# Six waits of TensorE, each preceded by 2 to 7 matmuls of the mask with the identity

## The chip, the cores and the metric

The kernel runs on one core of one Trainium2 chip. The metric is the device time in microseconds (us) of one execution; less is better. In the profile, PE is TensorE's matmuls, PEld its weight loads, DVE is VectorE, ACT is ScalarE, POOL is GpSimd and SP is SyncE.

## The reference

The input is `x` of 16 sequences (called b below) of 256 positions and 128 channels, fp32. Four layers follow one another. Each normalises x and adds two branches to it.

```python
# layer 0
x1 = mqa(xn) + xn                      # 16 heads of 8, one shared k and v, causal softmax
y  = mamba(x1)                         # conv over 4 steps, h = dA*h + dBu, y = sum_n h*C, gate, w_out
x  = x + (y + x1) + experts0(xn)       # 32 experts, each takes its 8 best positions
# layer 1
x  = x + attention(xn) + ffn(xn)       # 16 heads of 64; silu(fp4(x)@fp4(wg)) * (fp4(x)@fp4(wu)), then fp4(.)@fp4(wd)
# layer 2
x  = x + attention(xn) + switch(xn)    # 16 heads of 8; one of 8 experts for each position, with a capacity
# layer 3
x  = x + context(ssm_scan(xn)) + moe(xn)
```

## The kernel before

**The order of the work.** For each layer a Python program writes the queue of every engine by hand. A stage is a generator that yields a slot number before each piece of work, and `merge` puts the pieces of several stages into one queue in the order of their slots. One round of this is a turn, and a turn works on several sequences at once: in layer 0, turn t holds `pe_pre0(t+2)` (normalised input, gate, q, k, v), `pe_wide0(t)` (the scores of t and the row maxima of t+1), `pe_out(t-1)` and `pe_inner(t-1)` (output projection and the first half of mamba), `pe_states(t-2)` (the scan) and `pe_results(t-3)` (mamba's output). Layer 2 has turns of `pe_pre2`, `pe_wide` and `pe_out`; layer 1 has turns of attention, `pe_ffn` and the next sequence's projections. Each engine runs its queue in order and waits on semaphores; `wait_ge` leaves out a wait that its queue has already seen.

**Scores.** `pe_quad` makes the scores of four groups of heads at once, in two slots of two PSUM banks each, from operands with 8 rows (for the maxima, L569) or 9 rows (for the exponentials, L573: the ninth row carries the negated maximum). It then adds the causal mask by multiplying it with the identity into the same bank, in bf16 (L578 for the maxima, L580 for the keys). `k.slot_read` and `pe_take` (with `k.pre_read`) hold the event after which a bank may be written again.

**The six places.** In each, TensorE waits first or also for the bank, and then for operands.

- `pe_pre0`, slot 46 (layer 0): the bank is free when DVE has read q (L967); the operand is `gv`, the gate's values. Then L270 transposes them.
- `pe_quad` with the keys, first of three (layer 2): the bank is free after `mxT` was read by ACT (L1796), the operand is the negated maximum, which a DMA carries into the ninth row of q (`negmax`). Then L573.
- `pe_max_turn` (layer 2): the operand is the last of the row maxima `mx` (DVE, L1308). Then L597 turns them.
- `pe_pv`, half 0 (layer 0): the operands are the exponentials `pt` (ACT, L1787). Then L617 multiplies them with v.
- `pe_results` (layer 0): the operand is `yT` (DVE, L1452). Then L784 multiplies it with `w_out`.
- `pe_ffn`, q = 0 (layer 1): the operand is `xqT` (ACT, L1934). Then L832 and L833 make gate and up.

Two further pieces of layer 0 matter below. `pe_sums` (L761) adds the scan's states with the identity as weights, 16 matmuls on fp32 data that the trace shows in records of 256 columns each. DVE's products (L1417) write the scan's input from what L748 spreads, into the tiles that L761 reads.

Of the kernel before, what the change touches and what calls it, by code (L numbers as in the profile page):

```python
# [236 lines left out]
    return k.bank[PRE_BANK[l]]  # L237


def pe_pre0(k, b):  # L240
    pe, w = k.pe, k.w
    xn, xnT = k.xn[b % 3], k.xnT[b % 2]
    yield 17.2
    bk = pe_take(k, 0)
    pe.wait_ge(*k.at("xn", 0, b))
    for q in range(QT):
        i = pe.e.transpose(bk[:, q * P:(q + 1) * P], xn[:, q, :], w["ident"])
    i.then_inc(*k.set("xn_turned", 0, b))
    k.pre_read = ("xnT", 0, b)
    yield 18.6  # L250
    bk = pe_take(k, 0)
    pe.e.matmul(bk[0:E0, 0:L], w["gate_w"], xnT[:, :], start=True, stop=True).then_inc(*k.set("gate", b))
    k.pre_read = ("gz", b)
    yield 24
    bk = pe_take(k, 0)
    for g in (0, 1):
        i = pe.e.matmul(bk[:, g * L:(g + 1) * L], w["wq0"][:, g, :], xnT[:, :], start=True, stop=True)
    i.then_inc(*k.set("qk", 0, b, 0))
    k.pre_read = ("qk_act", 0, b, 0)
    yield 41  # L260
    bk = pe_take(k, 0)
    for g in (2, 3):
        i = pe.e.matmul(bk[:, (g - 2) * L:(g - 1) * L], w["wq0"][:, g, :], xnT[:, :], start=True, stop=True)
    i.then_inc(*k.set("qk", 0, b, 1))
    k.pre_read = ("qk_ve", 0, b, 1)
    yield 46
    bk = pe_take(k, 0)
    pe.wait_ge(*k.at("gv", b))
    for q in range(QT):
        i = pe.e.transpose(bk[:, q * E0:(q + 1) * E0], k.PT[:, b, q * P:(q + 1) * P], w["ident"][0:E0, 0:E0])  # L270
    i.then_inc(*k.set("gv_turned", b))
    k.pre_read = ("gvT", b)
    yield 48
    bk = pe_take(k, 0)
    for q in range(QT):
        i = pe.e.matmul(bk[:, 0:E0], xn[:, q, :], k.gvT[:, q, :], start=q == 0, stop=q == QT - 1)
    i.then_inc(*k.set("merged_mm", b))
    k.pre_read = ("merged", b)
    yield 51.1
    bk = pe_take(k, 0)  # L280
    pe.e.matmul(bk[:, 0:L], w["wk0"][:, 0, :], xnT[:, :], start=True, stop=True)
    for q in range(QT):
        i = pe.e.matmul(bk[:, L + 8 * q:L + 8 * q + 8], xnT[:, q * P:(q + 1) * P], w["wv0"], start=True, stop=True)
    i.then_inc(*k.set("v_mm", 0, b, 1))
    k.pre_read = ("v", 0, b)
# [262 lines left out]
def pe_quad(k, l, kind, b, c):  # L548

    pe, w, qT, kT = k.pe, k.w, k.qT[b % 3], k.kT[b % 3]  # L550
    slots, groups = quad_slots(l, kind, b, c), quad_groups(kind, c)
    nh = len(groups)
    wid = 512 // nh
    for s in slots:
        if k.slot_read[s] is not None:
            pe.wait_ge(*k.at(*k.slot_read[s]))
    if c == 0 and kind == "max":
        pe.wait_ge(*k.at("qk_act", l, b, (len(QK[l]) - 1) // 2 * 2))
        pe.wait_ge(*k.at("qk_ve", l, b, len(QK[l]) // 2 * 2 - 1))
        pe.wait_ge(*k.at("v", l, b))  # L560
    if c == 0 and kind == "keys":
        pe.wait_ge(*k.at(f"negmax{b % 2}", l, b))
    banks = [k.bank[2 * slots[r // 2] + r % 2] for r in range(4)]
    for n, g in enumerate(groups):
        for r in range(4):
            cols, kg, row = slice(n * wid, (n + 1) * wid), g if l else 0, 32 * r
            if kind == "max":
                q0 = P if nh == 2 else 0
                pe.e.matmul(banks[r][:, cols], qT[row:row + 8, g, q0:q0 + P], kT[row:row + 8, kg, 0:wid],  # L569
                            start=n == 0, stop=True, skip_group_check=True)  # L570
            else:
                k0 = 0 if nh == 2 else P
                pe.e.matmul(banks[r][:, cols], kT[row:row + 9, kg, k0:k0 + P], qT[row:row + 9, g, k0:L],  # L573
                            start=n == 0, stop=True, skip_group_check=True)
    for r in range(4):
        v3 = banks[r].rearrange("p (n x) -> p n x", n=nh)
        if kind == "max":
            i = pe.e.matmul(v3[:, :, wid - P:wid], w["identb"], w["mask"][:, 0:nh * P], start=False, stop=True, skip_group_check=True)  # L578
        else:
            i = pe.e.matmul(v3[:, :, 0:P], w["identb"], w["maskT"][:, 0:nh * P], start=False, stop=True, skip_group_check=True)  # L580
    i.then_inc(*k.set("quad_" + kind, l, b, c))
    for h in range(2):
        k.slot_read[slots[h]] = ("mx" if kind == "max" else "exp", l, b, c, h)
# [7 lines left out]
def pe_max_turn(k, l, b):  # L591
    pe = k.pe
    s = quad_slots(l, "keys", b, 0)[0]
    pe.wait_ge(*k.at(*k.slot_read[s]))
    pe.wait_ge(*k.at("mx", l, b, 2, 1))
    for q in range(QT):
        i = pe.e.transpose(k.bank[2 * s][0:HEADS, q * P:(q + 1) * P], k.mx[b % 2][:, q, :, :].rearrange("p r g -> p (r g)"), k.w["ident"])  # L597
    i.then_inc(*k.set("mx_turned", l, b))
    k.slot_read[s] = ("mxT", l, b)


def pe_pv(k, l, b, half):

    pe, v, bk = k.pe, k.v[b % 3], k.bank[OUT_BANK[l]]
    c = 2 * half
    pe.wait_ge(*k.at("exp", l, b, c, 1))
    pe.wait_ge(*k.at("exp", l, b, 1, 1))
    if half:
        pe.wait_ge(*k.at("oU", l, b, 0))
    elif b:  # L610
        pe.wait_ge(*(k.at("x1", l, b - 1) if l else k.at("zc", b - 1, 1)))
    for kb in range(2):
        for n in range(2):
            for r in range(4):
                g, o = 2 * half + n, (r % 2) * 512
                pt = k.pt[2 * c + r // 2][:, o + n * L:o + (n + 1) * L] if kb == 0 else k.pt[2 + r // 2][:, o + g * P:o + (g + 1) * P]
                i = pe.e.matmul(bk[32 * r:32 * r + 32, n * L + kb * P:(n + 1) * L], v[:, kb, 4 * g + r if l else 0, :], pt,  # L617
                                start=kb == 0 and n == 0, stop=kb == 1, tile_position=(0, 32 * r), skip_group_check=True)
    i.then_inc(*k.set("pv", l, b, half))
# [156 lines left out]
def pe_results(k, b):  # L776

    pe, w = k.pe, k.w
    yield 13.1
    bk = pe_take(k, 0)  # L780
    pe.wait_ge(*k.at("yT", b))
    for q in range(QT):
        for c in range(CI):
            i = pe.e.matmul(bk[:, q * P:(q + 1) * P], k.yT[:, c, q * P:(q + 1) * P], w["w_out"][:, c, :], start=c == 0, stop=c == CI - 1)  # L784
    i.then_inc(*k.set("y_out", b))
    k.pre_read = ("x_mamba", b)
# [26 lines left out]
def pe_ffn(k, b):  # L813
    pe, w = k.pe, k.w
    B6, B7 = k.bank[6], k.bank[7]
    yield 12.6
    pe.wait_ge(*k.at("fp4", "x", b))
    if b:
        pe.wait_ge(*k.at("x_ffn", b - 1))
        pe.wait_ge(*k.at("hqT", b - 1, 2))  # L820
    for q in range(QT):
        i = pe.e.transpose(B7[:, q * P:(q + 1) * P], k.xq[:, q, :], w["ident"])
    i.then_inc(*k.set("xq_turned", b))
    for q in range(QT):
        yield GATE1[q]
        if q == 0:
            pe.wait_ge(*k.at("xqT", b))
            if b == 0:
                pe.wait_ge(*k.at("x_spread", 1))
        else:  # L830
            pe.wait_ge(*k.at("hh", b, q - 1))
        pe.e.matmul(B6[:, 0:I1], k.xqT[:, q * P:(q + 1) * P], k.wgT[:, :], start=True, stop=True).then_inc(*k.set("gate1", b, q))  # L832
        pe.e.matmul(B7[:, 0:I1], k.xqT[:, q * P:(q + 1) * P], k.wuT[:, :], start=True, stop=True).then_inc(*k.set("up1", b, q))  # L833
    for ch in range(3):
        yield HQ1[ch]
        rows, bk = min(P, I1 - ch * P), B6 if ch % 2 == 0 else B7
        pe.wait_ge(*k.at("fp4", "h", b))
        if ch == 0 and b + 2 < NB:
            pe.wait_ge(*k.at("x_spread", b + 2))
        if ch == 2:  # L840
            pe.wait_ge(*k.at("hqT", b, 0))
        for q in range(QT):
            i = pe.e.transpose(bk[0:rows, q * P:(q + 1) * P], k.hq[:, q, ch * P:ch * P + rows], w["ident"])
        i.then_inc(*k.set("hq_turned", b, ch))
    yield 46
    pe.wait_ge(*k.at("hqT", b, 2))
    for q in range(QT):
        for ch in range(3):
            rows = min(P, I1 - ch * P)
            i = pe.e.matmul(B7[:, q * P:(q + 1) * P], k.hqT[0:rows, ch, q * P:(q + 1) * P], k.wdT[0:rows, ch, :], start=ch == 0, stop=ch == 2)  # L850
    i.then_inc(*k.set("down1", b))
# [1787 lines left out]
```

## Time and profile before

| | before |
|---|---|
| time, median of 3 runs | 3434.24 us (3432.38 to 3438.52) |
| span of the profiled execution | 3436.0 us |
| TensorE matmul busy (PE) | 2682.7 us, 78% |
| VectorE busy (DVE) | 2233.3 us, 65% |
| ScalarE busy (ACT) | 1430.7 us, 42% |
| GpSimd busy (POOL) | 834.9 us, 24% |
| mean granted TensorE clock | 0.812 |

The profiled execution has no time of its own beside its span of 3436.0 us, which is 1.8 us above the median of the runs and within their range. Layer 0 lies between about 30 and 1150 us of the span, its experts until about 1340, layer 1 until about 2270, layer 2 until about 2870, and layer 3 ends the span. A busy share of PE says how long matmuls were in flight, not how fast they ran: the same matmul is in flight for longer when the granted clock is low. [...]

### The profile page before, as it was taken

Reading aid. Unit: us, or ns where it says so; the run is one execution under the profiler, and the core shown is the slowest. Engines: PE = TensorE matmul, PEld = TensorE weight load, DVE = VectorE, ACT = ScalarE, POOL = GpSimd, SP = SyncE. Lnnn points to the kernel's source line nnn. Section 1 sums busy time; section 2 is a strip of 40 time slices with the busy share of each in tenths; the row PEclk is TensorE's granted clock in tenths of the full one; section 3 lists DMA queues with packets and bytes.
Section 4 is the critical chain, followed back from the end, with each engine's and each line's share of the span. In section 5 each row is a group of like instructions: output and inputs, shape, how many; then the busy total and the mean of one; then the engine's idle time right before and its main releaser. Section 6 shows DMA issues by size and latency. Waiting matters only on the chain.

```text
span 3436.0 us, 46802 instructions
## 1 busy us (share of the span) xinstructions
PE 2682.7 (78%) x17705; PEld 1913.2 (56%) x17705; DVE 2233.3 (65%) x4585; ACT 1430.7 (42%) x3688; POOL 834.9 (24%) x453
## 2 busy tenths in 40 slices
PE   4788888888886876878787877758888886677776
PEld 2466666666655774555555555535565555445444
DVE  3478888887878333656666666644544533899887
ACT  1334434434444003555555555512332323444443
POOL 0033333333344200222222222210000000333332
PEclk9778778778788656899989999966777768888887
DMA  1001100110101430000000000000000002443442
GB/s 54 20 32 34 36 32 30 40 32 26 44 32 44 137 141 1 1 1 1 1 1 1 1 1 1 1 33 17 25 17 12 6 16 63 148 144 125 149 137 87
DMA packets 71345, 147.93 MB, mean 43 GB/s; under 512 B 6864, under 2 KB 37072, under 8 KB 70608
## 3 DMA queue, kind: packets, MB, share of 16 engines
q1 hardware_dynamic: 69072, 140.73, 12.5%
q0 software_dynamic: 2048, 4.20, 0.4%
q8 instruction: 141, 2.31, 0.3%
q14 instruction: 84, 0.69, 0.1%
HBM read 135.20 MB, written 9.18 MB: 42 GB/s over the span
## 4 chain that ended last, share of the span: by engine, by line
PE 32%; DVE 15%; issue 12%; ACT 8%; POOL 5%; DMA 1%; SPq 0%; DVEq 0%; POOLq 0%; ACTq 0%
POOL h L2033 4%; ACT pr L1743 3%; PE psum L569 2%; PE psum L573 2%; PE psum L497 2%; PE psum L340 2%; DVE mx L1264 2%; PE psum L761 2%; PE psum L508 2%; PE psum L463 2%; PE psum L318 2%; PE psum L809 2%; PE psum L580 2%; PE psum L799 2%; PE psum L578 1%
## 5 line engine op out<-in xcount | busy, mean ns | idle before, releaser
L1999 POOL TENSOR_TENSOR h<-h,Crep 128x1024 f32<-128x1024 f32 x128 | 383.2, 3004 | 759.5 <-DVE h L1426 759.5
L1981 POOL TENSOR_TENSOR pr<-pr,rsum 128x512 f32<-128x512 f32 x192 | 228.0, 1191 | 756.2 <-DVE rsum L1276 756.2
L1308 DVE TENSOR_REDUCE mx<-psum 128x4 f32<-128x1024 f32 (+1 forms) x192 | 229.0, 1216 | 121.5 <-PE psum L578 121.5
L761 PE MATMUL psum<-h,pack_wf 128*128 128x256 f32 x1024 | 290.8, 448 | 5.4 <-POOL h L1999 5.4
L1426 DVE TENSOR_TENSOR_SCAN h<-dA,h 128x1024 f32<-128x1024 f32 x128 | 290.8, 2286 | 2.4 <-ACT dA L1884 1.8
L761 PEld LDWEIGHTS psum<-h,pack_wf 128*128 128x128 f32 x1024 | 236.5, 236 | 54.5 <-POOL h L1999 6.4
L1787 ACT ACTIVATE pt<-psum 128x1024 f32<-128x1024 f32 x192 | 187.4, 1021 | 146.5 <-PE psum L580 142.4
L1417 DVE TENSOR_TENSOR h<-dtu,psum 128x512 f32<-128x512 f32 x256 | 164.4, 676 | 117.1 <-PE psum L748 71.0
L2033 POOL TENSOR_TENSOR h<-h,Crep 128x1024 f32<-128x1024 f32 x64 | 150.6, 2354 | 350.2 <-DVE h L1185 350.2
L1743 ACT ACTIVATE pr<-psum,nb 128x256 f32<-128x256 f32 (+1 forms) x512 | 211.9, 441 | 31.2 <-DVE nb L1268 31.2
L1884 ACT ACTIVATE dA<-delta,A 128x255 f32<-128x255 f32 x512 | 210.2, 495 | 12.1 <-DVE h L1426 10.7
L395 PE MATMUL psum<-h,pack_wf 128*128 128x256 f32 x512 | 149.9, 444 | 55.5 <-POOL h L2033 54.8
L1753 ACT ACTIVATE prT<-psum 128x512 f32<-128x512 f32 x192 | 115.0, 599 | 181.2 <-PE psum L477 180.5
L573 PE MATMUL psum<-qT,kT 9*128 9x256 f32 (+1 forms) x2048 | 150.6, 439 | 50.1 <-DMA qT<-mxT 30.3
L313 PE MATMUL psum<-xnT,pack_wf 128*128 128x256 f32 x512 | 154.8, 429 | 21.6 <-ACT qT L1646 14.9
L569 PE MATMUL psum<-kT,qT 8*128 8x128 f32 (+1 forms) x2048 | 151.1, 432 | 25.9 <-ACT pt L1787 17.3
L395 PEld LDWEIGHTS psum<-h,pack_wf 128*128 128x128 f32 x512 | 106.5, 218 | 88.7 <-POOL h L2033 73.7
L573 PEld LDWEIGHTS psum<-qT,kT 9*128 9x128 f32 x2048 | 109.9, 259 | 79.2 <-issue 45.9
L2008 POOL DMA_INDIRECT slots<-xn,sloti x32 | 30.9, 967 | 503.4 <-DVE sloti L1101 498.6
L1185 DVE TENSOR_TENSOR_SCAN h<-dA,h 128x1024 f32<-128x1024 f32 x64 | 146.1, 2283 | 0.6 <-issue 0.3
L617 PE MATMUL psum<-pt,v 128*32 128x256 f32 (+1 forms) x2048 | 119.8, 384 | 28.3 <-ACT pt L1787 28.3
L1276 DVE RECIPROCAL rsum<-sums 128x2 f32<-128x2 f32 (+1 forms) x192 | 31.8, 166 | 167.2 <-ACT pr L1743 165.0
(339 smaller groups left out, 5881.6 us busy)
## 6 DMA issues: line engine op xcount, KB each, us to landing
Crep<-c_rows SPq DMA_DIRECT2D x64, 512.0 KB, 3.9
Brep<-bc_rows SPq DMA_DIRECT2D x64, 512.0 KB, 6.3
Crep<-bc_rows SPq DMA_DIRECT2D x64, 512.0 KB, 6.0
w1r<-m_w SPq DMA_DIRECT2D x32, 256.0 KB
w2r<-m_w SPq DMA_DIRECT2D x32, 256.0 KB
pack_wf<-wf SPq DMA_DIRECT2D x1, 3192.0 KB, 10.3
slots<-zero SPq DMA_DIRECT2D x12, 256.0 KB, 3.0
w1s<-s_w SPq DMA_DIRECT2D x8, 256.0 KB
```

Of the source, the lines that this page charges most:

```text
L395: i = pe.e.matmul(bk, k.w["ident"], k.h[g][:, n, :], start=g == 0 and n == 0, stop=g == 3 and n == NG - 1)
L569: pe.e.matmul(banks[r][:, cols], qT[row:row + 8, g, q0:q0 + P], kT[row:row + 8, kg, 0:wid], start=n == 0, stop=True, skip_group_check=True)
L573: pe.e.matmul(banks[r][:, cols], kT[row:row + 9, kg, k0:k0 + P], qT[row:row + 9, g, k0:L], start=n == 0, stop=True, skip_group_check=True)
L761: i = pe.e.matmul(YB[:, c * L:(c + 1) * L], w["ident"], h[:, n, :], start=g == 0 and n == 0 and c == 0, stop=g == 3 and n == NG - 1, skip_ ...
L1308: ve.e.tensor_reduce(mx[:, qb, 2 * h:2 * h + 2, groups[0]:groups[-1] + 1], k.psum[:, base:base + 2, :].rearrange("p i (n x) -> p i n x", n ...
L1426: ve.e.tensor_tensor_scan(flat(h), flat(k.dA[c][g % 2]), flat(h), 0.0, ALU.mult, ALU.add).then_inc(*k.set("scanned", 0, b, g, c))
L1743: i = ac.e.activation(pr[:, h * wid:(h + 1) * wid], bk[:, h * wid:(h + 1) * wid], ACT.Exp, bias=nb[:, h:h + 1], scale=float(HD[1]) ** -0.5 ...
L1787: ac.e.activation(k.pt[2 * c + h][:, :], k.psum[:, base:base + 2, :].rearrange("p i x -> p (i x)"), ACT.Exp, scale=float(HD[l]) ** -0.5).t ...
L1884: i = ac.e.activation(k.dA[c][g % 2][:, n, 1:], k.delta[x % 2][:, c, 1:], ACT.Exp, scale=k.A0[:, c, g * NG + n:g * NG + n + 1])
L1981: po.e.tensor_tensor(p3, p3, bcast(k.rsum[n][:, 0:len(heads[r])], P * (q + 1), 2), ALU.mult).then_inc(*k.set("normed", 1, b, p, r))
L1999: po.e.tensor_tensor(h[:, :, :], h[:, :, :], k.Crep[n % 3][:, :, :], ALU.mult).then_inc(*k.set("hC", 0, b, g, c))
L2033: po.e.tensor_tensor(k.h[g][:, :, :], k.h[g][:, :, :], k.Crep[g][:, :, :], ALU.mult).then_inc(*k.set("hC", 3, b, g))
```

## The change

A new function `pe_idle` issues n matmuls of the mask (bf16, 512 columns) with the identity (128 by 128) into a given bank. It is called at the six places, after the wait for the bank and ahead of the wait for the operands. What the matmuls write is overwritten by the work that follows, which starts its own accumulation. In `pe_pv` and `pe_ffn` the waits change order to make this possible, and in `pe_quad` the list of banks is made earlier. They add up to 16 times 2 + 4 + 5 in layer 0, 16 times 7 in layer 1 and 16 times 7 + 6 in layer 2, 496 matmuls in all.

```diff
+def pe_idle(k, bk, n):
+
+    for i in range(n):
+        k.pe.e.matmul(bk[:, :], k.w["identb"], k.w["mask"], start=True, stop=True, skip_group_check=True)
@@ pe_pre0
     yield 46
     bk = pe_take(k, 0)
+    pe_idle(k, bk, 2)
     pe.wait_ge(*k.at("gv", b))
@@ pe_quad
+    banks = [k.bank[2 * slots[r // 2] + r % 2] for r in range(4)]
     if c == 0 and kind == "keys":
+        if l:
+            pe_idle(k, banks[0], 7)
         pe.wait_ge(*k.at(f"negmax{b % 2}", l, b))
-    banks = [k.bank[2 * slots[r // 2] + r % 2] for r in range(4)]
@@ pe_max_turn
     pe.wait_ge(*k.at(*k.slot_read[s]))
+    if l:
+        pe_idle(k, k.bank[2 * s], 6)
     pe.wait_ge(*k.at("mx", l, b, 2, 1))
@@ pe_pv
-    pe.wait_ge(*k.at("exp", l, b, c, 1))
-    pe.wait_ge(*k.at("exp", l, b, 1, 1))
     if half:
         pe.wait_ge(*k.at("oU", l, b, 0))
     elif b:
         pe.wait_ge(*(k.at("x1", l, b - 1) if l else k.at("zc", b - 1, 1)))
+    if l == 0 and half == 0:
+        pe_idle(k, bk, 4)
+    pe.wait_ge(*k.at("exp", l, b, c, 1))
+    pe.wait_ge(*k.at("exp", l, b, 1, 1))
@@ pe_results
     bk = pe_take(k, 0)
+    pe_idle(k, bk, 5)
     pe.wait_ge(*k.at("yT", b))
@@ pe_ffn, q == 0
-            pe.wait_ge(*k.at("xqT", b))
             if b == 0:
                 pe.wait_ge(*k.at("x_spread", 1))
+            pe_idle(k, B6, 7)
+            pe.wait_ge(*k.at("xqT", b))
```

## Rows read from the trace of the kernel before

**Rows 1.** Busy time and granted clock (PEclk) of the steady turns of layers 0, 1, 2.
```profile
219.85:997.00 777.15, 680.76 (x4526) 494.35 (x4527) 631.93 (x873) 347.18 (x703) 287.63 (x97) 0.79 0.10 34
...
1360.00:2260.00 900.00, 711.10 (x5071) 509.38 (x5071) 576.59 (x1337) 504.32 (x1702) 221.54 (x186) 0.92 0.00 1
2355.00:2800.00 445.00, 378.16 (x3554) 257.89 (x3554) 220.96 (x727) 142.80 (x244) 26.88 (x28) 0.75 0.05 15
```
**Rows 2.** The same view, one turn of layer 0: PE, PEld, DVE, ACT, POOL, PEclk.
```profile
489.50:499.74 10.24, 7.95 (x67) 5.63 (x65) 9.53 (x17) 0.38 (x1) 6.54 (x2) 1.00 0.16 51
499.74:509.98 10.24, 8.87 (x39) 6.84 (x40) 8.52 (x10) 2.71 (x5) 4.29 (x2) 0.50 0.01 2
509.98:520.22 10.24, 7.87 (x41) 5.80 (x40) 5.17 (x7) 3.96 (x9) 0.43 (x1) 1.00 0.00 0
520.22:527.05 6.83, 6.83 (x44) 5.06 (x45) 5.33 (x11) 5.79 (x13) 0.10 (x1) 0.50 0.00 0
527.05:544.11 17.06, 16.21 (x139) 11.10 (x138) 15.45 (x22) 8.14 (x16) 9.64 (x3) 1.00 0.18 63
544.11:554.35 10.24, 9.20 (x57) 6.92 (x58) 9.03 (x12) 8.04 (x19) 3.06 (x2) 0.50 0.17 55
```
**Rows 3.** Timeline of PE, layer 0, from 499 us: start, length, idle before.
```profile
499.08 0.61 PE L580 MATMUL psum<-maskT,identb 128*128 128x256 bf16 x4
501.11 2.08 PE L784 MATMUL psum<-pack_wf,yT 128*128 128x128 f32 x8 [1.42 <-DVE yT L1452]
...
506.39 5.39 PE L761 MATMUL psum<-h,pack_wf 128*128 128x256 f32 x16
```
**Rows 4.** Groups of PE by line, layer 0, 219.85 to 1000 us: idle before, last releaser.
```profile
L617 PE MATMUL psum<-pt,v 128*32 128x256 f32 (+1 forms) x800 | 53.3, 425 | 16.8 <-ACT pt L1787 16.8
...
L784 PE MATMUL psum<-pack_wf,yT 128*128 128x128 f32 x96 | 24.9, 441 | 16.5 <-DVE yT L1452 16.5
...
L270 PE MATMUL psum<-pack_wf,PT 32*128 32x32 f32 x22 | 3.4, 232 | 5.4 <-DVE qT L967 5.4
```
**Rows 5.** Groups of DVE by line, layer 0, 219.85 to 997 us.
```profile
L1417 DVE TENSOR_TENSOR h<-dtu,psum 128x512 f32<-128x512 f32 x192 | 123.1, 676 | 90.6 <-PE psum L748 53.6 <-PE psum L761 36.9
L1308 DVE TENSOR_REDUCE mx<-psum 128x4 f32<-128x1024 f32 (+1 forms) x72 | 87.7, 1217 | 20.7 <-PE psum L578 20.7
```
**Rows 6.** Timeline of PE: the mask over 512 columns, clock 0.50.
```profile
522.12 1.89 PE L580 MATMUL psum<-maskT,identb 128*128 128x512 bf16 x4
```
**Rows 7.** Timeline of PE: the mask over 512 columns, clock 1.00.
```profile
2478.97 1.04 PE L578 MATMUL psum<-mask,identb 128*128 128x512 bf16 x4
2479.84 0.61 PE L346 MATMUL psum<-pack_wf,xnT 128*128 128x128 f32 x4
```
**Rows 8.** Timeline of PE, layer 0: the half 0 of `pe_pv`.
```profile
531.97 1.29 PE L617 MATMUL psum<-pt,v 128*32 128x256 f32 x24
```
**Rows 9.** Groups of PE by line, layer 2, 2355 to 2800 us.
```profile
L573 PE MATMUL psum<-qT,kT 9*128 9x256 f32 (+1 forms) x896 | 70.3, 463 | 27.5 <-DMA qT<-mxT 26.5 <-DVE mx L1308 1.0
...
L597 PE MATMUL psum<-pack_wf,mx 128*16 128x128 f32 x28 | 5.4, 275 | 22.8 <-DVE mx L1308 22.8
```
**Rows 10.** Timeline of ACT, layer 2: the read that frees the bank of the keys.
```profile
2452.72 0.37 ACT L1796 ACTIVATE mxT<-psum 16x256 f32<-16x256 f32 x1 [1.38 <-PE psum L597]
```
**Rows 11.** Timeline of PE, layer 2, after the wait for the negated maximum.
```profile
2455.08 1.65 PE L573 MATMUL psum<-qT,kT 9*128 9x256 f32 x16 [1.86 <-DMA qT<-mxT]
```
**Rows 12.** Busy time and granted clock, layer 2, one turn and more by the clock's level.
```profile
2438.51:2455.58 17.07, 13.25 (x175) 9.14 (x178) 11.64 (x42) 5.81 (x10) 0.18 (x1) 1.00 0.04 10
2455.58:2469.23 13.65, 12.92 (x88) 8.55 (x84) 4.57 (x13) 4.25 (x8) 1.74 (x2) 0.50 0.12 39
```
**Rows 13.** Groups of PE by line, layer 1, 1360 to 2260 us.
```profile
L832 PE MATMUL psum<-wgT,xqT 128*128 128x352 f32 x62 | 28.7, 547 | 52.9 <-ACT xqT L1934 37.4 <-DVE hh L1559 15.5
```
**Rows 14.** Timeline of PE, layer 1: gate and up of two sequences.
```profile
1475.85 1.47 PE L832 MATMUL psum<-wgT,xqT 128*128 128x352 f32 x2 [2.48 <-ACT xqT L1934]
...
1592.61 0.86 PE L832 MATMUL psum<-wgT,xqT 128*128 128x352 f32 x2 [2.48 <-ACT xqT L1934]
```

## The prediction

> **What bounds the kernel now.** I read the busy time and the granted clock by layer first. In the steady turns of layer 0 matmuls are in flight for 680.76 of 777.15 us, in layer 1 for 711.10 of 900, in layer 2 for 378.16 of 445, and the clock is granted at 0.79, 0.92 and 0.75 [rows 1]. TensorE is thus the fullest engine in all three, and part of its busy time comes from the low clock. DVE follows in layer 0 with 631.93 us.
>
> The second view cuts one turn of layer 0 at the points where the clock changed. The turn takes 64.85 us and has three stretches at 0.50, of 10.24, 6.83 and 10.24 us [rows 2]: 27.3 us, 42% of the turn. In them PE is busy for 8.87, 6.83 and 9.20 us, more fully than in the fast stretches around them. [...] The matmuls of the change have 128 rows and 128 columns of weights, the same form as the mask's own.
>
> The third view is who waits for whom. DVE's products L1417 are idle ahead of their start for 90.6 us in 12 turns, 7.6 us a turn, for matmuls (L748 and L761), its maxima L1308 for another 20.7 [rows 5]. In layer 0 a faster TensorE therefore moves DVE too, until these 9.3 us a turn are used up.
>
> **The price of one added matmul.** The mask over 512 columns is in the trace. At the high clock four start within 0.87 us (2478.97 to 2479.84) [rows 7], 0.22 us each. At the low one four take 1.89 us in place of 1.04 [rows 6, 7], 0.21 more each, so 0.43. All 496 cost between 109 and 213 us of TensorE's time; what counts is how much lies in waits.
>
> **yT, five matmuls (layer 0).** L784 waits 16.5 us in 12 turns, 1.37 each [rows 4]. L580 ahead of it ends at 499.69, and the clock falls at 499.74 [rows 2, 3]. Its bank was freed long before, so the five start at once: 1.09 us at the high clock, inside the wait, or 2.13 at the low one, 0.76 beyond it. I take the high one. The fall comes right where the score matmuls and the wait meet, and the first full matmul is ahead of it. What the fall costs now: 8.87 us of matmuls at the low clock [rows 2], 4.4 at the high one. Of the 4.4 gained I take off 0.7 as an estimate, a sixth, for waits on ScalarE and GpSimd that a faster TensorE meets: 3.7 us. As a check, L761 takes 5.39 us there [rows 3] and 16 times 0.22, 3.5, at the high clock; the other 1.8 come from what runs between 501.11 and 506.39. DVE can follow, since its products wait there for L761 and then L748.
>
> **Exponentials, four matmuls, and gv, two (layer 0).** The half 0 of `pe_pv` starts at 531.97 with no wait [rows 8]; the idle time of L617 (16.8 us in 13 turns) belongs to half 1. Here four matmuls cost 4 x 0.22 = 0.87 us in full, and DVE's L1308 next waits for TensorE's L578 [rows 5], so it moves the turn. At L270 the wait that ends last is the one for the bank, DVE's L967, 5.4 us in 11 turns [rows 4], and the two matmuls come after it. They add 0.43 ahead of L270, but behind it L617 waits 16.8/13 = 1.3 us for ScalarE, and that covers them. If that cover were gone they would cost 0.43 a turn. What they can give: the six lie in the 1 to 12 us ahead of the fall at 544.11. If it comes later, part of 9.20 us of matmuls in the slow stretch runs at half its time, at most 4.6; but DVE is busy for 9.03 of 10.24 us there [rows 2], so no more than 1.2 can be had. I take 1.2 - 0.87, a gain of 0.3; the bounds are a loss of 1.3 (0.87 + 0.43, no change of the clock) and a gain of 0.8 (the clock, and half of the 0.87 hidden).
>
> Layer 0: 3.7 + 0.3 = 4.0 us a turn in 12 turns, 48 us. The first two turns have no mamba results yet and the last three hold less work; I count nothing for them. Bounds: 12 x (2.0 + 0.8) = 34 and 12 x (-0.76 - 1.3) = -25 if no fall is moved, 12 x (4.4 + 0.8) = 62 at most.
>
> **Maxima, six, and negated maximum, seven (layer 2).** L597 waits 22.8 us in 14 turns, 1.63 each, and six take 1.31. The keys' L573 waits 26.5 us for the DMA of the maximum, 1.89 each [rows 9]. Its bank is freed at 2453.09 by the copy of mxT [rows 10], so the seven lie between 2453.09 and 2455.08 [rows 11], 1.99 us, and take 1.53. Both fit at the high clock; at the low one they take 2.56 and 2.98 and stick out by 0.9 and 1.0. The wait lies just ahead of the fall in each turn (here at 2455.58) [rows 12]. With the fall later, the scores and the mask behind the wait, about 3 us at the low clock, take 1.5; where the fall now comes inside them the gain is less. I take 1.1 us. [...] 15 turns x 1.1 = 16 us. Bounds: a loss of 15 x 1.9 = 28, and a gain of 15 x 2.5 = 38 if turns come to need one slow stretch less.
>
> **xqT, seven (layer 1).** Of the 37.4 us [rows 13] each wait holds 2.48 [rows 14], and seven take 1.53, hidden; 2.98 at the low clock would stick out by 0.5. Only where the wait lets the clock fall is there a gain: at 1475.85 L832 takes 1.47 us, at 1592.61 it takes 0.86 with the same wait ahead [rows 14]. L832 with what follows it loses about 1.5 us in such a turn. By the lengths of L832, which read 1.4 us or more or 0.86, it is 4 turns of 16: 6 us. Bounds: -8 and +12.
>
> **Sum.** 48 + 16 + 6 = 70 us. Against the execution with the span of 3436.0 us this gives 3366. The median of the runs is 1.8 us below that span, so 3364; I round to 3366.
>
> [...]
>
> **The rivals.**
>
> - *The clock falls as before, and the added matmuls only cost.* For it: the clock falls also without a wait, at 520.22, where PE is busy throughout the stretch [rows 2]. Against it: the six places lie right at falls. Price: layer 0 0.87 a turn, and half of 0.76 for yT, 12 x 1.25 = 15; layer 2 at the high clock nothing; 3451 us. It decides if the stretch after L580 at 499 is still at 0.50. Chance 0.09.
> - *The added matmuls run at the low clock and stick out of every wait.* 12 x 2.06 + 15 x 1.9 + 16 x 0.5 = 61 us: 3497. Chance 0.03.
> - *The gain in layer 0 is given back.* The turn is tied to the clock's steps: starting earlier, a turn meets the next fall elsewhere, and only layers 1 and 2 and a third of layer 0 gain: 16 + 6 + 16 = 38 us, about 3396 (3395 to 3426). Chance 0.2.
> - *Gain and loss balance*, within 0.2% (6.9 us, about what a measurement of this kernel can tell): the matmuls of half 0 and the shifted falls eat the rest. Chance 0.06.
> - *A faster TensorE meets DVE.* If all waits of DVE for PE went, layer 0 would gain 12 x 9.3 = 111 us, and layer 2 38: 3290 us. For that the slow stretch at 520.22 would have to go too, and nothing is added ahead of it. Chance 0.04.
> - The forecast itself, 3325 to 3395: 0.58.
>
> Faster 0.82, same 0.06, slower 0.12. The range goes from 3320 to 3426: it leaves out the slower and balanced cases (0.18) and the extreme below.
>
> **What would show it.** In layer 0 the turn, from one L784 to the next, falls from 64.85 to about 61 us, and the stretch behind L784 reads 1.00. L761 behind it takes about 3.6 us in place of 5.39. DVE's waits at L1417 shrink by a third or more. L617's half 0 starts 0.9 us after L748. In layer 2 L573 behind the DMA takes 1.15 us in place of 1.65, and the turn, 31.8 us on average (445 us hold 14), shortens by about 1. In layer 1 no L832 behind the wait takes 1.47 us. Layer 3 does not change. The prediction is wrong if the granted clock in layer 0 stays near 0.79, or if it rises and the turn stays, since then DVE or ScalarE would be the bound.

## The result

The changed kernel takes 3320.66 us (median of 4 runs, 3318.3 to 3331.45) against 3436.22 us (4 runs, 3432.38 to 3438.52). The ratio is 0.9677, with a 95% interval from 0.9651 to 0.9702: 3.2% or 116 us faster. The prediction was 3366 us with a range from 3320 to 3426. The direction came out; the gain was 70 us forecast against 116 measured, which is 0.7 us inside the end of the range. Beside the experiments below the kernel before ran 41 times more, 32 times in 3427 to 3451 us and 9 times in 3389 to 3408 us at a mean clock of 0.819 to 0.823 (0.806 to 0.819 in the others), a difference that no profile caught and whose cause is open; it widens the intervals of the ratios below, and against the mean of those nine, 3397 us, the changed kernel is still 2.3% faster.

The head of the page of the kernel after, busy time of each engine:

```profile
PE 2629.0 (79%) x18201; PEld 1845.5 (56%) x18201; DVE 2230.2 (67%) x4585; ACT 1429.1 (43%) x3688; POOL 834.4 (25%) x453
```

TensorE has 496 matmuls more and is busy for 54 us less, because the others ran at a higher clock. DVE, ACT and POOL are busy for as long as before, within 3 us. The mean clock rose from 0.812 to 0.866.

The layers' times here and below are worked out from the starts of the first matmuls of each stage in the trace, one profiled execution of each kernel. The text of layer 0 is the same in the changed kernel and five others below, and it ends between 1119.8 and 1127.7 us; unchanged it ends between 1153.2 and 1156.3 us in three. Differences of a few us between two layers' times therefore say little.

| us | layer 0 | layer 1 | layer 2 | layer 3 | span |
|---|---|---|---|---|---|
| before | 1153.2 | 1000.5 | 559.8 | 552.2 | 3436.0 |
| after | 1119.8 | 981.4 | 496.8 | 551.5 | 3320.1 |
| difference | -33.4 | -19.1 | -63.0 | -0.7 | -115.9 |
| forecast | -48 | -6 | -16 | 0 | -70 |

Layer 0's column runs from the start of the span to the first matmul of its experts, layer 1's from there on behind the experts (1271.6 us before) to the first matmul of layer 2, layer 2's to its experts, and layer 3's to the last matmul. The two stretches of experts between the layers, 168 us together, and the last 2.4 us are left out; each changed by less than 1 us.

Busy time and granted clock of steady turns of layers 0, 1 and 2 in the kernel after; they answer to [rows 1]:

```profile
433.50:925.00 491.50, 407.72 (x3114) 293.74 (x3113) 422.19 (x589) 232.03 (x472) 192.61 (x64) 0.94 0.10 36
1330.00:2170.00 840.00, 694.32 (x4975) 489.03 (x4971) 553.65 (x1297) 488.29 (x1656) 212.94 (x180) 0.94 0.00 1
2302.00:2640.00 338.00, 314.88 (x3310) 207.19 (x3309) 197.76 (x667) 125.45 (x219) 23.88 (x25) 0.91 0.06 19
```

The clock went from 0.79 to 0.94, from 0.92 to 0.94 and from 0.75 to 0.91; these are means of stretches that read 1.00 or 0.50, as the next view has them. In layer 0 DVE passes TensorE: it is busy for 86% of its turns now and TensorE for 83%, where it was 81% and 88% [rows 1].

One turn of layer 0 by the clock's level, the same view as [rows 2]:

```profile
479.36:482.77 3.41, 3.41 (x15) 3.08 (x14) 3.19 (x5) 3.41 (x9) 0.47 (x1) 0.50 0.41 144
482.77:493.01 10.24, 8.00 (x67) 5.91 (x67) 9.86 (x17) 0.46 (x2) 6.55 (x2) 1.00 0.17 56
493.01:496.42 3.41, 3.41 (x13) 2.12 (x12) 3.34 (x7) 2.25 (x4) 0.00 (x0) 0.50 0.01 5
496.42:540.80 44.38, 36.15 (x301) 25.67 (x300) 36.42 (x49) 22.84 (x47) 17.08 (x6) 1.00 0.07 25
```

The turn is 61.44 us in place of 64.85. Its time at the low clock fell from 27.3 to 6.8 us, yet the turn is only 3.4 us shorter. DVE's busy time in it is 52.8 us, 53.0 before.

### The profile page after: what moved, and what is told of

Its sections match the earlier page's. It is cut to its first block, busy times and chain, and to the rows that moved or that the text cites. A ratio compares the mean times of both kernels' runs of the same rounds, so it can differ in the third digit from the quotient of the medians.

```text
span 3320.1 us, 47741 instructions
## 1 busy us (share of the span) xinstructions
PE 2629.0 (79%) x18201; PEld 1845.5 (56%) x18201; DVE 2230.2 (67%) x4585; ACT 1429.1 (43%) x3688; POOL 834.4 (25%) x453
## 4 chain that ended last, share of the span: by engine, by line
PE 44%; DVE 23%; issue 14%; ACT 11%; POOL 5%; DMA 2%; SPq 0%; DVEq 0%; POOLq 0%; ACTq 0%
POOL h L2048 4%; PE psum L774 4%; PE psum L578 4%; DVE mx L1323 3%; DVE h L1441 3%; PE psum L582 3%; ACT pr L1758 3%; PE psum L587 2%; DVE h L1432 2%; PE psum L325 2%; PE psum L470 2%; PE psum L589 2%; PE psum L347 2%; DVE mx L1279 2%; PE psum L630 2%
## 5 line engine op out<-in xcount | busy, mean ns | idle before, releaser
L1323 DVE TENSOR_REDUCE mx<-psum 128x4 f32<-128x1024 f32 (+1 forms) x192 | 229.0, 1217 | 122.8 <-PE psum L587 122.8
L774 PE MATMUL psum<-h,pack_wf 128*128 128x256 f32 x1024 | 255.1, 406 | 5.4 <-POOL h L2014 5.4
L774 PEld LDWEIGHTS psum<-h,pack_wf 128*128 128x128 f32 x1024 | 207.9, 208 | 42.5 <-POOL h L2014 6.4
L402 PE MATMUL psum<-h,pack_wf 128*128 128x256 f32 x512 | 151.0, 446 | 52.7 <-POOL h L2048 51.8
L402 PEld LDWEIGHTS psum<-h,pack_wf 128*128 128x128 f32 x512 | 106.7, 219 | 86.1 <-POOL h L2048 71.0
L578 PE MATMUL psum<-kT,qT 8*128 8x128 f32 (+1 forms) x2048 | 126.3, 376 | 30.9 <-ACT pt L1802 22.4
L243 PE MATMUL psum<-mask,identb 128*128 128x512 bf16 x496 | 142.1, 424 | 7.9 <-DVE qT L982 7.4
L582 PE MATMUL psum<-qT,kT 9*128 9x256 f32 (+1 forms) x2048 | 128.2, 384 | 22.9 <-DVE mx L1323 19.9
L2023 POOL DMA_INDIRECT slots<-xn,sloti x32 | 30.8, 964 | 440.3 <-DVE sloti L1116 435.4
L470 PE MATMUL psum<-kT,qT 64*128 64x256 f32 (+1 forms) x1024 | 126.7, 387 | 13.1 <-ACT pr L1758 13.1
```

The source lines that it names most:

```text
L402: i = pe.e.matmul(bk, k.w["ident"], k.h[g][:, n, :], start=g == 0 and n == 0, stop=g == 3 and n == NG - 1)
L774: i = pe.e.matmul(YB[:, c * L:(c + 1) * L], w["ident"], h[:, n, :], start=g == 0 and n == 0 and c == 0, stop=g == 3 and n == NG - 1, skip_ ...
L1323: ve.e.tensor_reduce(mx[:, qb, 2 * h:2 * h + 2, groups[0]:groups[-1] + 1], k.psum[:, base:base + 2, :].rearrange("p i (n x) -> p i n x", n ...
```

## Where the time went in layer 0

The timeline of PE around the five matmuls ahead of L798 (L784 before); they answer to [rows 3]:

```profile
493.28 2.34 PE L243 MATMUL psum<-mask,identb 128*128 128x512 bf16 x5
495.42 1.54 PE L798 MATMUL psum<-pack_wf,yT 128*128 128x128 f32 x8
...
498.63 3.62 PE L774 MATMUL psum<-h,pack_wf 128*128 128x256 f32 x16
```

Here the prediction had the level wrong and the effect nearly right. The clock still falls at 493.01, just ahead of the five, so they run at 0.50. From 493.28 to 495.42 they take 2.14 us, the 2.13 of [rows 6, 7], and L798 no longer waits. But the clock comes back 3.41 us after the fall and not 10.24 us after it, so the sums (L774, L761 before) take 3.62 us in place of 5.39.

DVE's groups over the 12 turns from 247 us, as in [rows 5]:

```profile
L1432 DVE TENSOR_TENSOR h<-dtu,psum 128x512 f32<-128x512 f32 x192 | 122.4, 675 | 55.4 <-PE psum L761 50.5 <-PE psum L774 4.9
L1323 DVE TENSOR_REDUCE mx<-psum 128x4 f32<-128x1024 f32 (+1 forms) x70 | 85.2, 1217 | 30.9 <-PE psum L587 30.9
```

The wait for L774's sums went from 36.9 to 4.9 us. The wait for L761's spread (L748 before) went only from 53.6 to 50.5, and the maxima (L1323) wait 30.9 us in place of 20.7. In the view of who waits for whom, same stretch, PE waits for DVE's products:

```profile
PE psum L761 <- DVE h L1432: 56.4, 49, 1.8
```

The same wait (of L748 for L1417) was 21.5 us over 12 turns before; that of the weight loads went from 36.2 to 72.6. TensorE is ahead of DVE more often now, and each waits for the other in turn.

## Layers 1 and 2

In layer 2 the wait groups of PE answer to [rows 9], and the stretches by level to [rows 12]:

```profile
L582 PE MATMUL psum<-qT,kT 9*128 9x256 f32 (+1 forms) x848 | 52.2, 381 | 2.6 <-DMA qT<-mxT 2.2
...
L608 PE MATMUL psum<-pack_wf,mx 128*16 128x128 f32 x28 | 5.4, 275 | 3.2 <-DVE mx L1323 3.2
```
```profile
2506.88:2513.71 6.83, 6.83 (x50) 4.94 (x52) 1.58 (x5) 2.52 (x6) 0.00 (x0) 0.50 0.00 0
2513.71:2561.49 47.78, 43.99 (x506) 28.56 (x506) 31.04 (x105) 18.23 (x31) 3.82 (x4) 1.00 0.02 8
```

Both waits are filled: 26.5 us for the DMA became 2.2, and 22.8 for the maxima 3.2. The clock is high for 47.8 us at a stretch, more than a turn, and falls again at 2561.49 us. Before, each turn had a slow stretch of 13.7 to 20.5 us. Most turns last 25.6 and 28.8 us in alternation, but a pair in the middle takes 30.15 each, with a slow stretch of 10.24 us in each; over 14 turns the average is 27.7 us, where it had been 32.3.

In layer 1 the wait ahead of gate and up is filled too, and 0.97 us of it is left, about the 2.48 of [rows 14] less seven times 0.22:

```profile
1436.86 1.67 PE L243 MATMUL psum<-mask,identb 128*128 128x512 bf16 x7
1439.50 0.86 PE L847 MATMUL psum<-wgT,xqT 128*128 128x352 f32 x2 [0.97 <-ACT xqT L1949]
```

The longest of all 64 L847 is 0.56 us, so none ran at the low clock; the longest L832 took 0.96 before.

## The experiments

The ratios are each taken against the runs of the kernel before that stood beside the run in question.

**Theory 1** is that the added matmuls work by how much of the array they use (128 rows of operands, where the scores have 8 or 9), and that the higher clock is the whole gain. **Rival 2**: any matmul in flight does it. **Rival 3**: the changed order of waits does it. **Theory 4** (rival 4 in the first expectations): what layer 2 gains hangs on when it is reached. **Rival 5**, in the last three runs: DVE bounds the turn of layer 0 by now, not the clock.

### The same 496 matmuls with 8 rows

```diff
-        k.pe.e.matmul(bk[:, :], k.w["identb"], k.w["mask"], start=True, stop=True, skip_group_check=True)
+        k.pe.e.matmul(bk[:, :], k.w["identb"][0:8, :], k.w["mask"][0:8, :], start=True, stop=True, skip_group_check=True)
```

> All 496 matmuls stay in place and take the same time on TensorE, but use 8 of the 128 rows of the array. Theory 1 (how much of the array works is what holds the clock, and the higher clock is the whole gain): the clock falls as before, mean 0.81 or a little less, the turn of layer 0 goes back to about 65 to 66 us, and the time is 3436 to 3500 us, the before time plus what sticks out of the waits. Rival 2 (any matmul in flight in the wait holds the clock): the clock stays at 0.866 and the time at about 3321 us. Rival 3 (the gain comes from the changed order of waits in pe_pv and pe_ffn): also about 3321 us.

Measured: 3494.01 us, ratio 1.0226 (1.0131 to 1.0321). The timeline of PE, and then busy time and clock of its turns in layers 0 and 2:

```profile
553.22 1.03 PE L243 MATMUL psum<-mask,identb 8*128 8x512 bf16 x4
```
```profile
230.00:1030.00 800.00, 691.90 (x4486) 483.24 (x4501) 608.44 (x853) 337.17 (x684) 282.51 (x94) 0.81 0.10 32
...
2400.00:2800.00 400.00, 373.55 (x3326) 244.67 (x3343) 200.79 (x673) 128.52 (x222) 24.88 (x26) 0.75 0.06 17
```

Four of them at the high clock take 1.03 us, as four full ones do in the changed kernel (from 583.52 us of it), and stand in the same waits with the same order of waits. The clock stays at 0.81 in layer 0 and 0.75 in layer 2, layer 0's turn grows to 68.3 us (66.2 and 70.3 by turns), and layer 2 is at 567.1 us. The five ahead of L798 lie in a slow stretch of 17.07 us (585.68 to 602.75), where five full ones lie in one of 3.41. So rivals 2 and 3 fall for layers 0 and 2. For layer 1 they don't: it takes 992.5 us here, 8.0 of the 19.1 that it gains in the changed kernel, and one L847 behind the wait is slow where four L832 were. Whether matmuls of 8 rows, the order of waits or another meeting with the clock did that is not shown. The run also changes how many values other than zero the operands hold, and does not tell that from the number of rows.

This run is also the price of the added matmuls when the clock does not follow: 58 us by the medians, 52 in the profile, of which layer 0 has 52.4, layer 2 7.3 and layer 1 -8.0. The prediction gave its dearest rival 61 us, but as 25, 28 and 8; that the sums are near each other is luck.

PE is busy for 86% of layer 0's turns with 8 rows (691.90 of 800 us) and for 83% with 128 (407.72 of 491.50), yet the clock is 0.81 in the first and 0.94 in the second. In layer 2 it is 93% in both (373.55 of 400 and 314.88 of 338), at 0.75 and 0.91. Here the time in flight alone did not decide.

### One layer at a time

Each keeps the calls of one layer and sets n to 0 in the others.

```diff
-    pe_idle(k, bk, 2)
+    pe_idle(k, bk, 0)
```

> Only the 7 and 6 matmuls of layer 2 stay; layers 0 and 1 have none. Theory 1: layer 2 keeps the gain that its starts show in the changed kernel, 60 us, and layers 0 and 1 are as before, so 3376 us. Rival 4 (layer 2 gains so much only because the earlier layers deliver it at another point of the clock's steps): a good deal less than 60 us, 3395 to 3420 us.

> Only the 2, 4 and 5 matmuls of layer 0 stay. Theory 1: layer 0 alone gains 34 us, its turn is 61.44 us, time 3402 us. Rival 3 (order of waits) would give this too, but then the run with eight rows keeps it as well.

> Only the 7 matmuls in front of gate and up stay. Theory 1: layer 1 gains what its starts show in the changed kernel, 19 us, time 3417 us. If the 4 turns that had a slow L832 are all that it repairs, as the prediction had it, 6 us: 3430 us.

| matmuls kept in | time, us | ratio (95%) | layer 0 | layer 1 | layer 2 |
|---|---|---|---|---|---|
| layer 2 | 3412.37 | 0.9964 (0.9922 to 1.0006) | 1156.3 | 1000.5 | 539.4 |
| layer 0 | 3407.68 | 0.9977 (0.993 to 1.0024) | 1127.7 | 999.1 | 567.4 |
| layer 1 | 3425.48 | 1.0 (0.9957 to 1.0043) | 1156.1 | 987.4 | 563.0 |

None of the three ratios lies clear of 1; the gains are read from the layers' times in one profile each, of executions 6 to 10 us above their medians. By themselves the layers gain 20.4, 25.5 and 13.1 us, 59 of the 116. The medians, 24, 29 and 11 us below the 3436.22 of the result, say much the same. Layer 2 alone keeps a third of its gain: its turns are 30.7 us, one after the other, not 25.6 and 28.8. The time of 3412 us lies in the range of rival 4, and theory 1 as written, that each layer stands for itself, failed for layer 2. Layer 0 alone has six turns of 61.6 to 64.4 us before it settles on 61.4, and is 8 us short; the same text has two such turns in the changed kernel and four in the two runs of the next section, so this is not its being alone. Layer 1 alone gains 13 us, twice the forecast.

### One place at a time in layer 2

```diff
-        pe_idle(k, k.bank[2 * s], 6)
+        pe_idle(k, k.bank[2 * s], 0)
```

> The changed kernel without the six matmuls ahead of L608 (the row maxima) in layer 2; all else stays. Theory 1 (each place stands for itself by the array work it adds ahead of a fall): the seven ahead of the keys hold the clock alone, layer 2 takes 497 to 510 us, time 3321 to 3335. If layer 2's turns of 25.6 and 28.8 us need both places, layer 2 goes back to 540 us and the time to about 3364.

> The changed kernel without the seven ahead of the keys in layer 2. Here the wait for the DMA lets the clock fall again, so the scores behind it run at 0.50: layer 2 takes 530 to 560 us, time 3354 to 3384. If the six alone hold the clock, 500 us and 3323.

Without the six: 3367.16 us, ratio 0.9786 (0.9755 to 0.9818), layer 2 in 538.8 us with turns of 30.7. Without the seven: 3391.16 us, 0.9851 (0.9818 to 0.9884), layer 2 in 558.6 us with turns of 31.2 to 34.5, as before the change. The first is at the time expected if both places are needed, the second 7 us above its whole range of 3354 to 3384. So the seven alone give 21 us, the six alone about 1, and both together 63. They don't add up. But that the second step, from 30.7 us a turn to 25.6 and 28.8, needs both is not shown: three kernels with both in place, the one with layer 2 alone above and the two of the next section, also stay at 30.7.

### One part at a time in layer 0

> In layer 0 only the five ahead of yT's matmuls, none in layer 1, both places of layer 2. By the prediction the five carry 3.7 of 4.0 us a turn: layer 0's turn is 61.4 us and layer 0 ends near 1122 us. If instead the six at the exponentials and gv carry it, the turn stays at 64.85. Layer 2 is reached at another time than in the changed kernel: 497 us there if the arrival does not matter, 540 us as in the run with layer 2 alone if it does.

> In layer 0 only the four and the two matmuls, without the five ahead of yT's; layers 1 and 2 as in the changed kernel. By the prediction these two places gain 0.3 us a turn, so the turn is 64.5 to 65 us and layer 0 ends near 1150 us. If they carry the gain the turn is 61.4 us. Layer 2 again tells whether its time hangs on when it is reached: 497 or 540 us.

With the five alone (and none in layer 1) the time is 3381.73 us, ratio 0.9822 (0.9789 to 0.9856). Layer 0 ends at 1123.3 us, 29.9 of the 33.4 us; its turns are 61.1 to 63.0, 62.3 on average. The whole set of layer 0 ended between 1119.8 and 1127.7, so that what the other two places add to the five is not clear of the spread. With the four and the two alone (and layers 1 and 2 as changed) it is 3398.87 us, 0.9881 (0.9848 to 0.9914). Layer 0 ends at 1156.4 us, and its turns are 63.6 and 66.1, 64.85 on average as before, though the clock rose:

```profile
230.00:1000.00 770.00, 648.55 (x4573) 465.99 (x4577) 627.34 (x869) 344.17 (x698) 285.29 (x95) 0.87 0.10 34
```

So the four and the two raise the clock from 0.79 to 0.87 and gain no time by themselves. The likely reason, that what they cost lies on the path and DVE fills the stretch that gets faster, was not tested. The prediction gave them 0.3 us a turn and the five 3.7.

Both runs have the changed kernel's layer 2, to the letter, and it takes 536.1 and 537.0 us there with turns of 30.7 and 30.8, not 496.8. In the second of them the slow stretches are like this one:

```profile
2407.83:2418.07 10.24, 9.77 (x64) 6.65 (x56) 2.78 (x5) 2.62 (x7) 0.00 (x0) 0.50 0.01 2
```

Every turn has one such stretch. In the changed kernel one of 6.83 us comes every other turn, and two of 10.24 in the middle.

### Layer 2 reached 2 us later

```diff
-    for v in k.v:
-        k.ve.e.memset(v[:, :, :, 9:], 0.0)
-        k.ve.e.memset(v[:, :, :, 8:9], 1.0)
...
         q.wait_ge(*k.at(*landed("wf2")))
+    for v in k.v:
+        k.ve.e.memset(v[:, :, :, 9:], 0.0)
+        k.ve.e.memset(v[:, :, :, 8:9], 1.0)
```

> The changed kernel, with DVE's six memsets at the head of layer 2 moved behind the landing of its weights: the same work, but layer 2's turns begin some 2.3 us later against the clock's steps. Theory 4 (which rhythm layer 2 falls into hangs on when it is reached): its turns go to 30.7 us, layer 2 to about 540 us, time about 3366 us, 45 us for a delay of 2. If the arrival does not matter: 3323 us, turns of 25.6 and 28.8.

Measured: 3326.44 us, ratio 0.9674 (0.965 to 0.9697), layer 2 in 498.0 us. The delay was there: DVE's group of these memsets waits for the weights in this run.

```profile
L2393 DVE MEMSET v<- 128x736 f32 x2 | 1.3, 672 | 5.3 <-DMA pack_wf<-wf 5.2
```

The first turn grew from 28.2 to 29.4 us and the following ones fell into 25.6 and 28.8 as before. This expectation of theory 4 failed. Against the clock, layer 2 began 2.2 us later: 59.1 us ahead of the first fall in its turns, 61.3 in the changed kernel. The run with the four and the two alone began 61.4 us ahead of it, so at the same place, and took the other rhythm. That the same layer runs in two rhythms is shown by six runs; when it is reached did not decide between them.

The traces show where the two part. In that run and in the changed kernel each matmul of layer 2 starts within 0.05 us of its like, counted from the layer's first, up to the four matmuls of L643 at 86 us. The clock is at 1.00 in both. Then DVE goes on later (first pair of lines the changed kernel, second pair the other):

```profile
2306.45 0.60 PE L643 MATMUL psum<-pack_wf,oU 128*128 128x128 f32 x4
2307.08 0.26 DVE L1355 RECIPROCAL rs<-psum 128x16 f32<-128x16 f32 x1 [0.52 <-PE psum L643]
```
```profile
2343.91 0.60 PE L643 MATMUL psum<-pack_wf,oU 128*128 128x128 f32 x4
2345.16 0.26 DVE L1355 RECIPROCAL rs<-psum 128x16 f32<-128x16 f32 x1 [1.17 <-PE psum L643]
```

From the start of the fourth L643 to DVE's start it is 0.31 us in the first and 0.93 in the second. It is 0.31 us in every full turn of the three profiles that take 496.8 to 500.4 us, and 0.85 to 1.41 us in every one of the three that take 536.1 to 539.4. ScalarE's exponentials behind L589 start later by the same pattern (0.31 and about 1.0 us), and TensorE waits longer for them ahead of the next scores, 0.68 us in the first three and 1.00 to 1.63 in the others. The run without the six belongs to the second kind too (0.89 to 1.33 us). So the rhythms go with how soon the other engines start behind the same matmuls of TensorE there. What makes that differ between programs with the same text in this place is open, and no run changes it by itself.

### Three more in layer 2, six more in layer 0

```diff
 def pe_quad(k, l, kind, b, c):
     slots, groups = quad_slots(l, kind, b, c), quad_groups(kind, c)
+    if l and kind == "max" and c == 0 and b > 1:
+        pe_idle(k, pe_take(k, l), 3)
```
```diff
     i.then_inc(*k.set("merged_mm", b))
     k.pre_read = ("merged", b)
+    if b > 1:
+        s = quad_slots(0, "keys", b - 1, 0)[0]
+        pe.wait_ge(*k.at(*k.slot_read[s]))
+        pe_idle(k, k.bank[2 * s], 6)
```

> The changed kernel with three more matmuls of the mask in layer 2, into the free bank of the next projections, ahead of the wait for exponentials in front of the first maxima (0.7 us of idle time there, where the clock now falls next). Theory 1: the fall behind it goes too, turns near 25.6 us throughout, layer 2 in 450 to 470 us, time 3275 to 3295 us. If DVE and ScalarE bound the turn of layer 2 by now, 3315 to 3325. If the three stick out and move no fall: 3325 to 3335.

> The changed kernel with six more in layer 0, behind L283 and ahead of the wait of 1.8 us for DVE in front of L761. Theory 1 in its bare form (the clock is the bound): the remaining falls near 541 and 554 go, the turn drops below 60 us, layer 0 ends 20 us or more earlier. Rival 5 (DVE bounds the turn of layer 0 by now, it is busy through that wait): the clock of layer 0 rises from 0.93 but the turn stays within 1 us of 61.4, time 3310 to 3325 unless layer 2 is reached at a bad point (then 3360).

> Both additions together: the sum of the two gains, 3265 to 3295 us by theory 1; by rival 5 the time of the run with more in layer 2 alone, within 5 us.

| more in | time, us | ratio (95%) | layer 0 | layer 2 | clock in layer 2's turns |
|---|---|---|---|---|---|
| (changed kernel) | 3320.66 | 0.9677 (0.9651 to 0.9702) | 1119.8 | 496.8 | 0.91 |
| layer 2 | 3308.22 | 0.9619 (0.9593 to 0.9645) | 1123.3 | 483.4 | 0.95 |
| layer 0 | 3319.19 | 0.9653 (0.9631 to 0.9676) | 1119.5 | 500.4 | 0.91 |
| both | 3308.75 | 0.9627 (0.9605 to 0.965) | 1121.3 | 483.2 | 0.94 |

Three more in layer 2 take 13 us off it; by theory 1 it was to be 27 us or more. The turn is 27.3 us, one like the other, with one slow stretch of 3.41 us; the last four are 25.6 and have none. The stretch by level:

```profile
2425.35:2428.76 3.41, 3.41 (x10) 2.24 (x9) 0.14 (x1) 1.14 (x3) 0.00 (x0) 0.50 0.00 0
```

The three end at 2448.2 us and the next fall is at 2452.65. The fall moved behind them and became shorter, but did not go in most turns. In layer 0 the six more change neither the turn, 61.4 to 61.5 us, nor the clock, 0.94: the two slow stretches of 3.41 us became one of 6.83 (548.52 to 555.34). Theory 1's turn below 60 us did not come, but since the clock did not rise either, the run does not test rival 5, and what bounds this turn is open. Both together take the time of the run with three more in layer 2, within 1 us. That kernel is the fastest of the study, 0.4% below the changed one: its four executions, 3302 to 3313 us, lie below the changed kernel's 3318 to 3331, and the layer takes 483.4 and 483.2 us in two profiles.

## Why the prediction was right, and where it was off

What held is that matmuls of 128 rows in these waits raise the clock and that shorter turns follow; the run with 8 rows shows it for layers 0 and 2 (0.94 and 0.91 with 128 rows, 0.81 and 0.75 with 8, turns of 61.44 against 68.3 us in layer 0, layer 2 in 496.8 us against 567.1). The total came inside the range by 0.7 us. The forecast was of the right sign for each layer, and off in size for all: layer 0's gain was put 15 us too high, layer 1's 13 and layer 2's 47 us too low. Three kernels above have the same layer 2 and take about 40 us longer there; in that rhythm the gain would be some 75 us by an estimate from these times, near the 70. So which rhythm the changed kernel fell into, which the prediction did not foresee, carries much of the distance, and that the time is still inside the range is luck.

That matmuls in a wait put off the fall was the author's estimate, on which the gains of all three layers rest; no row of before shows it. What the trace of before shows of the three falls of [rows 2], beside the wait of 1.42 us from 499.69 on [rows 3]:

```profile
520.13 2.05 PE L573 MATMUL psum<-qT,kT 9*128 9x128 f32 x32 [0.83 <-DVE mx L1308]
...
544.99 2.79 PE L617 MATMUL psum<-pt,v 128*32 128x256 f32 x32 [1.23 <-ACT pt L1787]
```

The clock falls at 499.74, 0.05 us into the first wait, at 520.22, 0.09 us behind the second, and at 544.11, in the third. So the fall at 520.22, which the first rival takes for one without a wait, has one of 0.83 us just ahead. But the wait of 1.15 us ahead of L635 at 495.63 passed at 1.00. Nor is PE busier in each slow stretch than in the fast ones beside it: 95% from 527.05 to 544.11 at 1.00 (16.21 of 17.06 us), 90% in the slow one behind it.

- *The price of a matmul*, 0.22 us at the high clock and 0.43 at the low one, held: seven took 1.67 us to the end of the last, and five at the low clock 2.14.
- *The five ahead of yT's matmuls carry layer 0*: right, 29.9 of 33.4 us with them alone. "I take the high one" was wrong: they run at the low clock and no longer fit the wait. They don't keep the clock from falling, but it comes back 6.83 us earlier (3.41 us after the fall, 10.24 before the change, 17.07 with 8 rows). The term of 3.7 us a turn measured 2.6 alone (64.85 to 62.3), and 3.4 with the rest.
- *The four and two*: forecast a gain of 0.3 us a turn, measured 0 alone; on top of the five the steady turn is 0.9 shorter, the end of the layer not clearly earlier.
- *Layer 0 as a whole*: 48 forecast, 33 measured, at the edge of the bounds of 34 and 62, for whose 2.0 us no source is given. The first turns, counted at nothing, lost time: the first L798 comes at 247.4 us where L784 came at 241.7 (245.0 with layer 0 unchanged and only layer 2 filled). From there to the last one the changed kernel gains 39 us.
- *Layer 2*: 16 forecast, 63 measured, beyond even the bound of 38. The step that failed is that each turn keeps its slow stretch, which the 1.1 us a turn suppose. It is kept in the runs where the turn is 30.7 us (10.24 us of each turn with the four and the two alone), and there the gain is 20 to 24 us, near the forecast. In the changed kernel the clock passes most second turns without a fall. The prediction read one turn's stretches and did not ask what becomes of the next turn when this one is shorter. Its turn of 31.8 us was also too short: 14 turns take 451.7 us, 32.3 each.
- *Layer 1*: 6 forecast, 19 measured (13 with nothing else changed). No L847 is slow any more, as said, but the price was taken for the four slow turns alone. Behind the first, the turns are 57.0 and 55.7 us in alternation now, 1.2 us less on average than the 57.5 before. Why the others got shorter too is not shown.
- *The rivals that only cost* were priced at 15 and 61 us. The run with 8 rows costs 58, nearly all of it in layer 0, where the prediction had put at most 25.
- *The waits*: in the whole trace before, those at the six places get longer than the rows shown: up to 2.1 us at L784 and 2.8 at L617, and 3.83 once, ahead of the first L832 at 1358.37 us.

Open is what makes DVE and ScalarE start sooner or later behind the same matmuls in layer 2, and with it the choice between the two rhythms, and what bounds layer 0 now.

## What to carry to other kernels

When TensorE's clock is low in the stretches where it is busiest, look at what ran just ahead of each fall: here it was waits of 0.83 to 1.42 us, with scores of 9 rows near them. Filling a wait that was there anyway with matmuls of 128 rows into the bank that is written next was cheap where they fit the wait: layer 1's 2.48 us took seven, with 0.97 us left. Six more in layer 0 changed nothing: 61.4 to 61.5 us a turn at 0.94 with and without them. Layer 2 ran in two rhythms, of 30.7 us a turn and of 25.6 and 28.8 in alternation, so measure such a change in the whole kernel and with its neighbours: here the parts add up to half of the whole. When two kernels with the same text in a layer differ there, lay their traces side by side from the layer's first matmul and look for the first instruction that is late.

## What the runs showed of the hardware that was not expected

- Matmuls of the same time in flight (1.03 us for four) with 8 rows in place of 128 did not hold the clock in layer 0: 0.81 against 0.94.
- Steady turns took on lengths that repeat to 0.1 us for eight turns and more: 64.85, 61.44, 30.7 and 27.3 us; 25.6 in alternation with 28.8 holds for seven. The slow stretches within them began at the same place of each turn: eight times 61.44 us after their like from 417.91 us on in the changed kernel's layer 0, twelve times 30.7 us from 2346.4 us on in layer 2 with the four and the two alone. The change moved layer 0's turn from 64.85 to 61.44 us; the four and the two alone moved it not at all, the clock rose from 0.79 to 0.87 with the mean turn still 64.85.
- The same text of layer 2 took 496.8 to 500.4 us in three profiles (the changed kernel, the one reached later, the one with more in layer 0) and 536.1 to 539.4 in three others. DVE follows the same four matmuls of TensorE 0.31 us after the last one's start in each turn of the first three, and 0.85 to 1.41 us after it in the others.
